# Six stack transfers a group in place of twelve: heads innermost in the scratch, stack rows ordered by part

## The chip, the cores and the metric

One core of one Trainium2 chip runs the whole program. The metric is device time in microseconds (us) of that core, the median of several executions.

## The reference

Eight sequences of 512 rows with 256 features pass through an attention layer and a mixture-of-experts layer, each followed by a layer norm. Cut to what matters here:

```python
qkv = (x @ qkv_w.T + qkv_b).reshape(B, T, 3, H, dh)          # B 8, T 512, H 16, dh 16
q, k, v = ...                                                # (B, H, T, dh) each
scores = where(causal, -inf, einsum('bhtd,bhsd->bhts', q, k) * dh ** -0.5)
seq_out = einsum('bhts,bhsd->bhtd', softmax(scores), v)
gated = mean over heads of sigmoid(memory_score * mem_scale) * sigmoid(x @ memg_w.T + memg_b)
x = layernorm(x + (seq_out + gated * mem_val) @ out_w.T + out_b)
x = layernorm(x + top2_experts_of_8(x))                      # float32 throughout
```

The memory score is a decayed running sum over products of "lines" computed from x; it is a side path of the kernel that runs on POOL and DVE.

## The kernel before, in words

**Arithmetic of the scores.** Float32 accuracy comes out of bf16 matmuls: q and k are each split into three bf16 parts (0 the coarsest), and of the nine products of parts six are kept. They are summed by the contraction itself. For one head the tile `Q` holds 96 rows (`STACK`): 16 features times six copies, where `Q_PARTS` names the part of q in each copy; `K` has the same rows with `K_PARTS`. One 96-row matmul of `Q` against `K` then gives the score. In `Q` two more rows, 96 and 97, hold the row maxima as two bf16 parts, against rows of -1 in `K`, so the transposed scores come out with the maximum already taken off.

**Projection.** For batch b+1, PE computes eight slices j (`pe_project`, L382). j = 0 to 3 are 128 channels of q or k each, (64 channels, or four heads, are one group; q of groups 0 and 1 is j = 0, k of them j = 1, and j = 2, 3 are groups 2 and 3). ACT writes part 0 into `HL` (L427), DVE the rest into `R` (L501), ACT part 1 (L438), POOL part 2 (`pool_third`, L632). SP stores the 128 x 3 x 512 bf16 slice in DRAM, `qk_scratch` (`sp_projected`, L642). j = 4 to 7 are v and memory values; the latter are stored by L645.

**Stacking.** `sp_stack` (L647 to L657) reads the scratch back, once for each copy: for tensor t (0 for Q, 1 for K) and each of six copies r it fills rows r, r+6, r+12, ... of the tile, 16 rows of four heads of 512 values. That is twelve transfers of 64 KB a group. It waits until the exp scores of the same group in the batch before are done (`s_st`), because they read the rows that it overwrites, and until the slice has landed in the scratch (`s_scr`).

**Attention.** A batch has four groups g, and a group has twelve units u. For each unit PE does the "exp scores" (L334: transposed scores with the maximum off), which ACT turns into probabilities (L419), POOL masks (L626) and PE multiplies with V (L345). Eight units ahead PE does the "max scores" (L322), and DVE takes the masked maximum of each row (L491). When the maxima of a group are complete, PE turns them (L365), ACT and DVE split them into `MT` (L452, L507), and SP copies `MT` into rows 96 and 97 of `Q` (`sp_max_rows`, L662). The first exp score of a group waits for these (`s_mrow`).

**Order on SP.** Every transfer of the program is issued by SP, in an order written out by hand (`sp_batch`). Beside the compute of batch b: in g = 0 the stack of group 3 of b, the load of x for b+2, MT of (b,1), slice 0 of b+1; in g = 1 the Q stack of (b+1,0), slice 1, MT of (b,2), the K stack of (b+1,0), slice 2; in g = 2 the stack of (b+1,1), slices 3 and 4, MT of (b,3), slice 5; in g = 3 the stack of (b+1,2), slice 6, MT of (b+1,0), slice 7. The semaphore of each piece is waited for in this order, so a late piece holds up what follows.

**Opening and end.** Before batch 0 (`opening`) PE projects batch 0 and all sixteen tiles of the memory lines (L238); SP stores these (L275), loads further x, stores the slices, and issues all four stacks of batch 0, then MT of (0,0). After batch 7 a third part, without any stack, does the output projection, norms and experts (`phase3`, PE L1296).

Of the kernel before, what the change touches and what calls it, by code (L numbers as in the profile page):

```python
# [8 lines left out]
BF16 = mybir.dt.bfloat16  # L9
# [5 lines left out]
P = 128  # L15
# [2 lines left out]
LEAD = 8  # L18
GROUP = 4
STACK = 96  # L20
Q_PARTS, K_PARTS = (0, 0, 1, 1, 0, 2), (0, 1, 0, 1, 2, 0)
TERMS = len(Q_PARTS)
VW = 17
NEG = -1e30
EPS = 1e-5
# [7 lines left out]
def need(eng, sem, per, b, c, least=1, apart=False):  # L33


    if isinstance(b, int):
        if per * b + c > 0:
            eng.wait_ge(sem, per * b + c)
    else:
        assert per * least + c > 0  # L40
        value = eng.to_reg(b * per + c)
        if apart:
            eng.wait_ge(sem, 1)
        eng.wait_ge(sem, value)


def build(nc, xT, x, qk_wT, qk_b, vc_wT, memv_w, memv_bT, out_wT, mem_wT, v_b, memg_b, mem_scale, decay_logits,
          iter_mix, out_b, gate_wT, gate_b, expert_w, expert_b, out):
    NB, _, KT, T = xT.shape
    D = KT * P  # L50
    QT = T // P
    H = memg_b.shape[0] // NB
    DH = D // H
# [5 lines left out]
    PU = NG * UNITS  # L59
    assert (NB, KT, T, H, DH, NG, NE) == (8, 2, 512, 16, 16, 4, 8)  # L60

    qk_scratch = nc.dram_tensor("qk_scratch", [NB, 4, P, 3, T], BF16, kind="Internal").ap()
    mem_scratch = nc.dram_tensor("mem_scratch", [NC, NB, H, T], F32, kind="Internal").ap()
    mv_scratch = nc.dram_tensor("mv_scratch", [NB, QT, P, D], F32, kind="Internal").ap()
    o_scratch = nc.dram_tensor("o_scratch", [NB, QT, P, D], F32, kind="Internal").ap()
# [1 line left out]
    with ExitStack() as ctx:  # L67
        def sb(name, shape, dt=F32, scope=ctx):
            return scope.enter_context(nc.sbuf_tensor(name, shape, dt))

        def sem(name):
            return ctx.enter_context(nc.semaphore(name))
# [41 lines left out]
        HL = sb("HL", [P, 2, 3, T], BF16, part2)  # L114
        Q = sb("Q", [P, H, T], BF16, part2)
        K = sb("K", [P, H, T], BF16, part2)
# [55 lines left out]
        s_scr = [sem(f"s_scr{i}") for i in range(4)]  # L172
        s_mvst = [sem(f"s_mvst{i}") for i in range(2)]
        s_stack = [sem(f"s_stack{i}") for i in range(NG)]
# [117 lines left out]
        def unit_parts(u):  # L292

            if u < 4:
                return 0, [u]
            if u < 8:
                return 1, [u - 4]
            return (2, [2 * (u - 8), 2 * (u - 8) + 1]) if u < 10 else (3, [2 * (u - 10), 2 * (u - 10) + 1])
# [13 lines left out]
        def pe_max_scores(pe, b, g, u):  # L312
            rank, heads = unit_parts(u)
            i = QT - 1 - rank
            n = P * (i + 1)
            if u == 0:
                need(pe, s_stack[g], 32 * TERMS, b, 32 * TERMS)
            need(pe, s_max, PU, b, UNITS * g + u - 2)
            for c, h in enumerate(heads):
                hh = GROUP * g + h  # L320
                o = S_ps[u % 3][:, c * 256:c * 256 + n]
                last = nc.tensor.matmul(o, Q[0:STACK, hh, P * i:P * i + P], K[0:STACK, hh, 0:n], start=True, stop=True)  # L322
            last.then_inc(s_s, 1)
# [65 lines left out]
        def pe_batch(pe, b, first=False, last=False):  # L389
            for g in range(NG):  # L390
                pb, pg = (b, g - 1) if g else (b - 1, NG - 1)
                for u in range(UNITS):
                    pe_exp_scores(pe, b, g, u)
                    on, ng, nu = ahead(g, u)
                    if not (last and on):
                        pe_max_scores(pe, b + on, ng, nu)
                    if u in (2, 6) and not (first and g == 0):
                        for kt in ((0, 1) if u == 2 else (2, 3)):
                            pe_values(pe, pb, pg, kt)
                    if u in (4, 10) and not last:  # L400
                        pe_project(pe, b + 1, 2 * g + u // 10)
                    if u == UNITS - LEAD and not (last and g == NG - 1):
                        pe_turn_max(pe, b + (g + 1) // NG, (g + 1) % NG)
                    if u == 10 and not (first and g == 0):
                        pe_turn_out(pe, pb, pg)
                    if last and (g, u) == (2, 8):
                        pe_gates(pe)
                    if last:
                        last_phase["tensor"]["beside"](pe, g, u)
# [229 lines left out]
        def sp_projected(sp, b, j):  # L639
            if j < 4:  # L640
                need(sp, s_h3, 4, b, j + 1, apart=True)
                sp.dma_start(qk_scratch[b, j], HL[:, j % 2]).then_inc(s_scr[j], 16)  # L642
            else:
                need(sp, s_hi, 8, b, j + 1, apart=True)
                sp.dma_start(mv_scratch[b, j - 4], MV[:, j % 2, :]).then_inc(s_mvst[j % 2], 16)  # L645

        def sp_stack(sp, b, g, which=(0, 1)):  # L647

            need(sp, s_st, PU, b, UNITS * (g + 1) - PU, apart=True)
            r0 = GROUP * DH * (g % 2)  # L650
            for t in which:
                j = 2 * (g // 2) + t
                need(sp, s_scr[j], 16, b, 16, apart=True)
                src = qk_scratch[b, j][r0:r0 + GROUP * DH].rearrange("(h d) s t -> s d h t", h=GROUP)
                for r, part in enumerate((Q_PARTS, K_PARTS)[t]):
                    sp.dma_start((Q, K)[t][r:STACK:TERMS, GROUP * g:GROUP * g + GROUP, :],  # L656
                                 src[part]).then_inc(s_stack[g], 16)  # L657

        def sp_max_rows(sp, b, g):
            need(sp, s_mt, 2 * NG, b, 2 * (g + 1), apart=True)  # L660
# [8 lines left out]
        def sp_batch(sp, b, first=False, last=False, more=True, read_rows=None):  # L669
            for g in range(NG):  # L670
                if g == 0 and not first:
                    sp_stack(sp, b, NG - 1)
                if g == 1 and not last:
                    sp_stack(sp, b + 1, 0, (0,))
                if g > 1 and not last:
                    sp_stack(sp, b + 1, g - 1)
                if g in (1, 2) and not last:
                    sp_projected(sp, b + 1, 2 * g - 1)
# [5 lines left out]
                if g > 1 and not last:  # L684
                    sp_projected(sp, b + 1, 2 * g)
# [4 lines left out]
                if not last:  # L690
                    sp_projected(sp, b + 1, 2 * g + (g > 1))
# [334 lines left out]
        def _(pe):  # L1026
# [20 lines left out]
            def scores(u0):  # L1047
                if u0 == 0:
                    for c in range(2):
                        pe.wait_ge(s_p1e[c], 3)  # L1050
                    pe.wait_ge(s_wr, 4)
                for u in range(u0, u0 + 3):
                    pe_max_scores(pe, 0, 0, u)
# [6 lines left out]
            for u in range(LEAD):  # L1060
                pe_max_scores(pe, 0, 1, u)
# [623 lines left out]
```

## Time and profile before

| | us |
|---|---|
| median of 3 runs (821.67 to 824.83) | 822.56 |
| the profiled execution, its own time | 823.05 |
| span of the profiled execution | 821.3 |
| PE busy (share of span) | 687.0 (84%) |
| DVE busy | 586.8 (71%) |
| POOL busy | 453.3 (55%) |
| ACT busy | 367.2 (45%) |
| granted TensorE clock, mean | 0.938 |
| stack transfers: 192 to Q and 192 to K, 64 KB each, issue to landing | 2.3 each |

PE is the matmul engine, PEld its weight load, DVE, ACT and POOL the three elementwise engines; SPq is the queue from which SP issues transfers. A transfer is issued by SP, cut into packets by hardware and moved by 16 DMA engines; "landing" is when its completion is seen. Busy shares are averages over stages with different limits: where one engine waits for another is read from the timelines and the chain.

### The profile page before, as it was taken

How to read it: one execution, taken by the hardware profiler on the slowest of the kernel's cores; microseconds unless marked ns; L12 is line 12 of the kernel's file. 1: busy time of each engine (PE TensorE's matmuls, PEld its weight loads, DVE VectorE, ACT ScalarE, POOL GpSimd, SP SyncE). 2: the span in 40 equal slices, each digit the busy share in tenths (PEclk: the TensorE clock that was granted, in tenths of full speed). 3: DMA queues.
4: the chain of work that ended last, by engine and by line, in shares of the span. 5: the costliest groups of instructions: out<-in, count | busy, mean ns of one | idle time of the engine just before them, and what ended most of it. 6: DMA issues, size and time to landing. Idle time of an engine off the chain costs nothing.

```text
span 821.3 us, 12578 instructions
## 1 busy us (share of the span) xinstructions
PE 687.0 (84%) x4004; PEld 421.6 (51%) x4004; DVE 586.8 (71%) x1946; ACT 367.2 (45%) x790; POOL 453.3 (55%) x365
## 2 busy tenths in 40 slices
PE   5992877978887888888888887779999899998995
PEld 2440443434444444444444442547677677776774
DVE  2443755956989887988888676546778777787785
ACT  3311644645656555655556465633323242232411
POOL 5200599998887786978987971514224043151410
PEclk9996898989999999999999997888999999999998
DMA  7665435233443332433433436030230311303000
GB/s 251 210 220 156 164 114 187 94 110 92 130 129 112 109 112 85 139 109 120 135 85 98 125 104 193 1 103 4 74 103 1 102 42 62 103 1 103 26 27 26
DMA packets 75445, 85.44 MB, mean 104 GB/s; under 512 B 11994, under 2 KB 64628, under 8 KB 75380
## 3 DMA queue, kind: packets, MB, share of 16 engines
q1 hardware_dynamic: 75380, 84.64, 32.9%
q8 instruction: 32, 0.52, 0.3%
q14 instruction: 33, 0.27, 0.1%
HBM read 54.72 MB, written 29.62 MB: 103 GB/s over the span
## 4 chain that ended last, share of the span: by engine, by line
PE 37%; DVE 22%; SPq 12%; POOL 12%; ACT 6%; issue 6%; DMA 4%; ACTq 0%; POOLq 0%; DVEq 0%
PE ps L1296 16%; SPq L656 9%; PE ps L382 5%; DVE ps L491 4%; PE ps L345 4%; PE ps L334 4%; DVE Ob L530 3%; DVE A L1430 3%; PE ps L322 2%; PE ps L1261 2%; ACT Pr L419 2%; POOL Pr L626 2%; ACT X L1282 2%; DMA Q<-MT 1%; DVE Z L1316 1%
## 5 line engine op out<-in xcount | busy, mean ns | idle before, releaser
L491 DVE CUSTOM_DVE_ANT_0 ps<-ps,mask 128x256 f32<-128x256 f32 (+3 forms) x512 | 237.8, 511 | 109.8 <-PE ps L322 108.3
L419 ACT ACTIVATE Pr<-ps 128x512 f32<-128x512 f32 (+2 forms) x384 | 183.9, 522 | 95.1 <-PE ps L334 94.1
L334 PE MATMUL ps<-Q,K 98*128 98x256 bf16 (+3 forms) x512 | 141.0, 320 | 61.1 <-DMA Q<-MT 34.8
L1296 PE MATMUL ps<-ew_hi,XT 128*128 128x512 f32 x512 | 176.6, 403 | 0.0
L322 PE MATMUL ps<-K,Q 96*128 96x256 bf16 (+3 forms) x512 | 138.6, 317 | 27.1 <-DVE nmax L491 26.2
L626 POOL TENSOR_SCALAR_AFFINE_SELECT Pr<-Pr 128x512 f32<-128x512 f32 x128 | 95.9, 763 | 113.2 <-ACT Pr L419 111.9
L1430 DVE SCALAR_TENSOR_TENSOR A<-ps,cw,A 128x256 f32<-128x256 f32 x256 | 123.6, 483 | 47.6 <-PE ps L1296 34.8
L334 PEld LDWEIGHTS ps<-Q,K 98*128 98x128 bf16 x512 | 46.0, 101 | 137.8 <-ACT Pr L419 68.7
L1296 PEld LDWEIGHTS ps<-ew_hi,XT 128*128 128x128 f32 x512 | 97.3, 190 | 21.1 <-issue 0.3
L1234 POOL TENSOR_TENSOR A<-A,X 128x512 f32<-128x512 f32 x16 | 20.6, 1288 | 149.3 <-ACT A L1288 149.3
L1296 PE MATMUL ps<-ew_rest,XT 128*128 128x512 f32 x256 | 101.7, 397 | 0.0
L345 PE MATMUL ps<-Pr,V 128*17 128x512 f32 (+3 forms) x1024 | 90.0, 471 | 0.2
L322 PEld LDWEIGHTS ps<-K,Q 96*128 96x128 bf16 x512 | 51.9, 103 | 63.7 <-issue 23.8
L491 DVE DVE_READ_ACCUMULATOR2_ANT nmax<- 128x1 f32 x512 | 70.3, 137 | 0.0
L1296 PEld LDWEIGHTS ps<-ew_rest,XT 128*128 128x128 f32 x256 | 48.7, 190 | 8.6
L632 POOL TENSOR_TENSOR HL<-R,HL 128x512 bf16<-128x512 f32 x32 | 38.9, 1215 | 25.2 <-ACT HL L438 24.2
L530 DVE TENSOR_TENSOR_SCAN Ob<-sc,Ob 128x512 f32<-128x512 f32 x36 | 49.8, 1383 | 1.0 <-POOL Ob L876 1.0
L382 PE MATMUL ps<-xhi,wqk 128*128 128x512 f32 x128 | 47.2, 453 | 3.2 <-DVE xlo L524 3.2
L345 PEld LDWEIGHTS ps<-Pr,V 128*17 128x17 f32 x1024 | 24.2, 101 | 48.8 <-issue 34.1
L427 ACT ACTIVATE HL<-ps,qkb 128x512 bf16<-128x512 f32 x32 | 22.0, 687 | 58.9 <-PE ps L382 52.2
L382 PE MATMUL ps<-wvc,xhi 128*128 128x512 f32 x128 | 45.2, 434 | 1.1 <-DVE bc L986 1.1
L882 POOL TENSOR_TENSOR Ob<-Ob,Rl 128x1533 f32<-128x1533 f32 x12 | 34.8, 2903 | 18.2 <-DVE Ob L530 18.2
(191 smaller groups left out, 1095.9 us busy)
## 6 DMA issues: line engine op xcount, KB each, us to landing
qk_scratch<-HL SPq DMA_DIRECT2D x32, 384.0 KB, 2.6
Q<-qk_scratch SPq DMA_DIRECT2D x192, 64.0 KB, 2.3
K<-qk_scratch SPq DMA_DIRECT2D x192, 64.0 KB, 2.3
Pr<-xT SPq DMA_DIRECT2D x8, 512.0 KB, 5.7
xraw<-xT SPq DMA_DIRECT2D x8, 512.0 KB, 3.8
mem_scratch<-Rl SPq DMA_DIRECT2D x16, 256.0 KB, 3.4
mv_scratch<-MV SPq DMA_DIRECT2D x32, 128.0 KB, 2.1
Wm<-mem_scratch SPq DMA_DIRECT2D x2, 2048.0 KB, 9.2
```

The lines of the kernel that those rows point to most:

```text
L322: last = nc.tensor.matmul(o, Q[0:STACK, hh, P * i:P * i + P], K[0:STACK, hh, 0:n], start=True, stop=True)
L334: last = nc.tensor.matmul(o, K[0:STACK + 2, hh, P * kt:P * kt + P], Q[0:STACK + 2, hh, T - n:T], start=True, stop=True)
L345: last = nc.tensor.matmul(O_ps[32 * h:32 * h + VW, P * kt:T], V[b % 2][:, kt, GROUP * g + h, :], probs(g % 2, kt, h, 1)[:, 0, :], start=(k ...
L382: last = nc.tensor.matmul(J_ps[:], lhs, rhs, start=first, stop=(j < 4 and k == KT - 1 and a == 1))
L419: nc.scalar.activation(probs(g % 2, kt, heads[0], len(heads)), src, ACT.Exp, scale=SCALE).then_inc(s_exp, 1)
L491: last = nc.vector.tensor_tensor_reduce(out=scores, in0=scores, in1=mask[:, T - w:T], scale=1.0, scalar=NEG, op0=ALU.add, op1=ALU.max, acc ...
L530: nc.vector.tensor_tensor_scan(Ob[:, j % 3, :], col(SC_D).to_broadcast([P, T]), Ob[:, j % 3, :], 0.0, ALU.mult, ALU.add).then_inc(s_scan, 1)
L626: nc.gpsimd.affine_select(out=diagonal, in_=diagonal, compare_op=ALU.is_ge, fill=0.0, base=0, pattern=[[0, GROUP], [1, P]], channel_multip ...
L632: nc.gpsimd.tensor_tensor(HL[:, j % 2, 2, :], R[:, j % 2, :], HL[:, j % 2, 1, :], ALU.subtract).then_inc(s_h3, 1)
L656: sp.dma_start((Q, K)[t][r:STACK:TERMS, GROUP * g:GROUP * g + GROUP, :], src[part]).then_inc(s_stack[g], 16)
L1296: last = nc.tensor.matmul(o, lhs(c, k), rhs(d, k), start=first, stop=(k == KT - 1 and c == 1))
L1430: ins = nc.vector.scalar_tensor_tensor(acc, F_ps[v % 4][:, D * c:D * c + D], cw[:, par, i, e:e + 1], acc, ALU.mult, ALU.add)
```

## The change

The scratch gets the part index outermost, so that a part of a slice is a block of 128 rows of 512 values. The host reorders the weight rows and biases of q and k, so that within a group the feature comes first and the head last: four heads of one feature are then 4 KB in one piece. The stack's rows are ordered by part (Q: part 0 three times, part 1 twice, part 2 once, 16 rows each; K: parts 0, 1, 2, then 0, 1, then 0), which are the same six products. For each of Q and K one transfer now fills 48 rows, one 32 and one 16. Q's repeats its source block 3, 2 and 1 times, K's reads 3, 2 and 1 consecutive blocks. The store into the scratch has rows of 1 KB in the scratch in place of 3 KB.

```diff
--- before.py
+++ after.py
@@ -18,8 +18,7 @@
 LEAD = 8
 GROUP = 4
 STACK = 96
-Q_PARTS, K_PARTS = (0, 0, 1, 1, 0, 2), (0, 1, 0, 1, 2, 0)
-TERMS = len(Q_PARTS)
+TERMS = ((0, 3), (1, 2), (2, 1))
 VW = 17
 NEG = -1e30
 EPS = 1e-5
@@ -59,7 +58,7 @@
     PU = NG * UNITS
     assert (NB, KT, T, H, DH, NG, NE) == (8, 2, 512, 16, 16, 4, 8)
 
-    qk_scratch = nc.dram_tensor("qk_scratch", [NB, 4, P, 3, T], BF16, kind="Internal").ap()
+    qk_scratch = nc.dram_tensor("qk_scratch", [NB, 4, 3, P, T], BF16, kind="Internal").ap()
     mem_scratch = nc.dram_tensor("mem_scratch", [NC, NB, H, T], F32, kind="Internal").ap()
     mv_scratch = nc.dram_tensor("mv_scratch", [NB, QT, P, D], F32, kind="Internal").ap()
     o_scratch = nc.dram_tensor("o_scratch", [NB, QT, P, D], F32, kind="Internal").ap()
@@ -314,7 +313,7 @@
             i = QT - 1 - rank
             n = P * (i + 1)
             if u == 0:
-                need(pe, s_stack[g], 32 * TERMS, b, 32 * TERMS)
+                need(pe, s_stack[g], 96, b, 96)
             need(pe, s_max, PU, b, UNITS * g + u - 2)
             for c, h in enumerate(heads):
                 hh = GROUP * g + h
@@ -639,7 +638,7 @@
         def sp_projected(sp, b, j):
             if j < 4:
                 need(sp, s_h3, 4, b, j + 1, apart=True)
-                sp.dma_start(qk_scratch[b, j], HL[:, j % 2]).then_inc(s_scr[j], 16)
+                sp.dma_start(qk_scratch[b, j].rearrange("s p t -> p s t"), HL[:, j % 2]).then_inc(s_scr[j], 16)
             else:
                 need(sp, s_hi, 8, b, j + 1, apart=True)
                 sp.dma_start(mv_scratch[b, j - 4], MV[:, j % 2, :]).then_inc(s_mvst[j % 2], 16)
@@ -651,10 +650,13 @@
             for t in which:
                 j = 2 * (g // 2) + t
                 need(sp, s_scr[j], 16, b, 16, apart=True)
-                src = qk_scratch[b, j][r0:r0 + GROUP * DH].rearrange("(h d) s t -> s d h t", h=GROUP)
-                for r, part in enumerate((Q_PARTS, K_PARTS)[t]):
-                    sp.dma_start((Q, K)[t][r:STACK:TERMS, GROUP * g:GROUP * g + GROUP, :],
-                                 src[part]).then_inc(s_stack[g], 16)
+                src = qk_scratch[b, j][:, r0:r0 + GROUP * DH].rearrange("s (d h) t -> s d h t", h=GROUP)
+                row = 0
+                for part, n in TERMS:
+                    dst = (Q, K)[t][row:row + n * DH, GROUP * g:GROUP * g + GROUP, :]
+                    parts = src[part:part + 1].to_broadcast([n, DH, GROUP, T]) if t == 0 else src[0:n]
+                    sp.dma_start(dst, parts).then_inc(s_stack[g], 16)
+                    row += n * DH
 
         def sp_max_rows(sp, b, g):
             need(sp, s_mt, 2 * NG, b, 2 * (g + 1), apart=True)
@@ -1652,13 +1654,14 @@
     B, T, D = x.shape
     H = L0_attn_memg_b.shape[0]
     qkv_w, qkv_b = np.asarray(L0_attn_qkv_w), np.asarray(L0_attn_qkv_b)
+    turned = np.arange(2 * D).reshape(2 * H // GROUP, GROUP, D // H).transpose(0, 2, 1).reshape(-1)
     lines = [np.stack([np.asarray(w).reshape(H, 4, D) for w in two], 1).reshape(8 * H, D)
              for two in ((L0_attn_w1w, L0_attn_w2w), (L0_attn_r1w, L0_attn_r2w))]
     arrays = {
         "xT": lay(x.transpose(0, 2, 1).reshape(B, D // P, P, T).transpose(0, 2, 1, 3)),
         "x": lay(x.reshape(B, T // P, P, D)),
-        "qk_wT": lay(qkv_w[:2 * D].T),
-        "qk_b": lay(qkv_b[:2 * D].reshape(4, P).T),
+        "qk_wT": lay(qkv_w[turned].T),
+        "qk_b": lay(qkv_b[turned].reshape(4, P).T),
         "vc_wT": lay(qkv_w[2 * D:].T),
         "memv_w": lay(np.asarray(L0_attn_memv_w)),
         "memv_bT": lay(np.asarray(L0_attn_memv_b).reshape(D // P, P).T),
```

## Rows read from the trace of the kernel before

**Rows 1.** The page: span, busy share of PE, chain that ended last

```profile
PE 687.0 (84%) x4004; PEld 421.6 (51%) x4004; DVE 586.8 (71%) x1946; ACT 367.2 (45%) x790; POOL 453.3 (55%) x365
...
PE ps L1296 16%; SPq L656 9%; PE ps L382 5%; DVE ps L491 4%; PE ps L345 4%; PE ps L334 4%; DVE Ob L530 3%; DVE A L1430 3%; PE ps L322 2%; PE ps L1261 2%; ACT Pr L419 2%; POOL Pr L626 2%; ACT X L1282 2%; DMA Q<-MT 1%; DVE Z L1316 1%
```

**Rows 2.** The chain from 25 to 82 us, its summary by line

```profile
by line: SPq L656 53.8%; SPq L275 12.0%; issue 8.2%; SPq L645 4.2%; SPq L279 3.6%; PE ps L238 3.0%; DMA Q<-MT 3.0%; SPq L285 2.3%; DVE xlo L524 2.2%; POOL HL L632 2.0%; ACT xhi L457 1.9%; ACT HL L438 1.1%; PE ps L334 1.1%; SPq L662 1.0%; SP
```

**Rows 3.** Timeline of PE: start, us, engine, line, names, count, [idle before <-releaser]

```profile
79.53 0.61 PE L334 MATMUL ps<-Q,K 98*128 98x512 bf16 x1 [11.40 <-DMA Q<-MT]
...
139.28 0.61 PE L334 MATMUL ps<-Q,K 98*128 98x512 bf16 x1 [4.21 <-DMA Q<-MT]
...
186.51 0.58 PE L334 MATMUL ps<-Q,K 98*128 98x512 bf16 x1 [1.85 <-DMA Q<-MT]
...
240.99 0.39 PE L334 MATMUL ps<-Q,K 98*128 98x512 bf16 x1 [0.97 <-DMA Q<-MT]
...
298.44 0.61 PE L334 MATMUL ps<-Q,K 98*128 98x512 bf16 x1
...
354.21 0.39 PE L334 MATMUL ps<-Q,K 98*128 98x512 bf16 x1 [1.68 <-DMA Q<-MT]
...
408.50 0.39 PE L334 MATMUL ps<-Q,K 98*128 98x512 bf16 x1 [0.98 <-DMA Q<-MT]
...
465.56 0.39 PE L334 MATMUL ps<-Q,K 98*128 98x512 bf16 x1 [2.78 <-DMA Q<-MT]
...
490.26 0.55 PE L334 MATMUL ps<-Q,K 98*128 98x512 bf16 x1 [1.90 <-DMA Q<-MT]
```

**Rows 4.** Timeline of SP's queue, same columns

```profile
77.14 1.22 SPq L662 DMA_DIRECT2D Q<-MT  x2
...
225.37 3.79 SPq L656 DMA_DIRECT2D K<-qk_scratch  x6
...
280.13 3.80 SPq L656 DMA_DIRECT2D K<-qk_scratch  x6
...
392.83 3.80 SPq L656 DMA_DIRECT2D K<-qk_scratch  x6
...
406.08 1.21 SPq L662 DMA_DIRECT2D Q<-MT  x2
...
447.60 3.80 SPq L656 DMA_DIRECT2D K<-qk_scratch  x6
```

**Rows 5.** By stretch, groups 2, 3 of batch 5: PE, PEld, DVE, ACT, POOL

```profile
393.52:408.50 14.98, 12.09 (x84) 6.14 (x83) 13.49 (x43) 8.40 (x21) 13.02 (x7) 1.00 0.45 143
408.50:420.72 12.22, 11.46 (x83) 6.41 (x84) 9.62 (x33) 6.94 (x17) 9.64 (x9) 1.00 0.31 86
```

**Rows 6.** Line L656, its Q transfers: issue ns min/median/max

```profile
L656 SPq DMA_DIRECT2D Q<-qk_scratch x192: 555/596/1723, 29.9 to 483.4; - x192
```

**Rows 7.** Line L662, the transfers of MT: issue to landing

```profile
DMA to landing us min/median/max: 1.6/1.7/7.2
```

**Rows 8.** Transfer view, whole span: packets, and the transfers of few rows

```profile
DMA packets 75445, 85.44 MB, mean 104 GB/s; under 512 B 11994, under 2 KB 64628, under 8 KB 75380
...
eb_raw<-expert_b SPq DMA_DIRECT2D x3, 8.0 KB
eb_raw<-out_b SPq DMA_DIRECT2D x2, 1.0 KB
```

**Rows 9.** Transfer view, 145.2 to 146.1 us: an xT load alone

```profile
DMA packets 82, 0.34 MB, mean 373 GB/s; under 512 B 0, under 2 KB 0, under 8 KB 82
...
q1 hardware_dynamic: 82, 0.34, 93.9%
```

**Rows 10.** Transfer view, 29.5 to 41 us: busy tenths, packets

```profile
DMA  9899999999999999999471520262424333256999
...
DMA packets 1707, 2.79 MB, mean 243 GB/s; under 512 B 272, under 2 KB 1040, under 8 KB 1706
...
q1 hardware_dynamic: 1706, 2.77, 72.1%
```

## The prediction

> **What bounds the kernel now.** I read the page first. PE is busy 84% of the span, and the chain that ended last is PE with one queue in it: SP's issue of line 656 holds 9% [rows 1]. A queue's issue is on a chain only where SP is late, so I asked where. The chain from 25 to 82 us says it: line 656 has 53.8% of that stretch [rows 2]. SP issues 48 stack transfers one behind another, gets to the first row maxima (MT) at 77.14 us, and PE, which had stopped 11.40 us before, starts the exp scores at 79.53 [rows 3, 4]. In the batches PE's timeline shows the same wait with smaller numbers, mostly at the start of g = 3: 1.85, 0.97, 1.68, 0.98 and 2.78 us in batches 1, 2, 4, 5, 6, none in batch 3; also 4.21 at batch 1's start and 1.90 at (7,1) [rows 3]. Between these waits PE is nearly full (11.46 of 12.22 us in group 3 of batch 5 [rows 5]). So the kernel is bound by PE with SP's order just beside it: MT of (5,3) is issued at 406.08, its second half some 0.6 us later, and PE starts at 408.50 [rows 3, 4]. Whoever shortens or lengthens what lies ahead of MT on SP and its rings moves these points and little else. Nothing after batch 7 is touched.
>
> **The change, part by part.** *Fewer issues.* An issue of line 656 takes 0.596 us [rows 6], so a group costs SP 6 x 0.6 = 3.6 us less. This is a gain only where MT was behind the stack. In the opening 24 x 0.6 = 14.3 us fall away, more than the 11.40 that PE waits. Behind stack issues are also the waits of 4.21, 1.85, 0.97, 1.68, 0.98 and 1.90. The wait of 2.78 in batch 6 has, in SP's listing, an idle stretch of SP for POOL's part 2 of slice 3 just ahead, so I give it nothing. The most to be won is 11.40 + 4.21 + 1.85 + 0.97 + 1.68 + 0.98 + 1.90 = 23.0 us.
>
> *Larger packets.* Alone, an xT load moved 82 packets of 4 KB in 0.9 us at 93.9% of 16 engines: 16 x 0.9 x 0.939 / 82 = 0.165, and I take 0.16 us a packet for one engine, or 26 KB a us [rows 9]. Packets of mixed sizes (1.6 KB on average) took 16 x 11.5 x 0.721 / 1707 = 0.078 us each [rows 10]. A 1 KB packet is thus between 0.04 (a quarter of 0.16) and 0.078. The stack's volume is unchanged; the store's 24 packets of 1 KB on each engine cost 1.0 to 1.9 us in place of 1.0 for eight of 3 KB. I take 1.0, since the 0.078 holds waiting too; the other end adds 0.9 to a store that mostly lies beside other work.
>
> *How many engines carry a transfer.* This decides. Before, the leading index of each stack transfer, on both sides, has 16 values (the features). After, the source's leading index is the copy or the part, with 3 values, then 2; only the third transfer, where it is 1 and drops out, leads with 16 again. What the trace has on this: packets under 512 B number 11,994, and by the code 2,176 of them are data (1,024 of MT, 384 of the gate's weights and biases, 512 scalars, 256 of two small biases). The other 9,818 are completion writes. The program issues 617 transfers; 16 each would make 9,872. The 54 missing are just those of the few-row transfers: three of 8 rows lack 8 each, two of one row lack 15 each [rows 8]. So a transfer runs on as many engines as its leading index gives, up to 16. No row shows 48 destination rows under a leading 3; I carry the count over. If it holds, the first transfer runs on 3 engines with 16 packets each and the second on 2 with 16 each, and the engine that has both, with 1 of the third, has 33 packets: 33 x 0.16 = 5.3 us for one tensor, 10.6 for Q and K, where 12 transfers of 4 KB an engine took 12 x 0.16 = 1.9 us of each engine. I assume that the shared engine is the same one each time; every 16-row transfer uses it too, and MT, whose 16 packets lie one on each engine, comes in last behind it.
> The Trainium skill (DMA: Bandwidth & Descriptors, "Why a DMA increments its semaphore by 16 and not by 1" and "Rules for kernel authors") says the same more sharply: the engine count is the largest up to 16 that divides the slowest dimension of both sides, on the lowest-numbered engines, and a leading broadcast of c copies confines a transfer to at most c. By that rule, the trace's 54 missing writes agree; the 3 and 2 here are its consequence, which no run here shows yet.
>
> *What that does to MT.* A small transfer takes 1.7 us to land [rows 7], 0.1 more to PE: I put 1.8 us of fixed time on the path of issue, packets and landing. That MT waits behind its ring is in the trace: one took 7.2 us [rows 7], the one behind the 2 MB load at 129 us. In g = 2 the path begins with the K stack of (b+1,0), issued at 392.83 in batch 5, 15.7 us before group 3 starts [rows 3, 4]. On the busy engine there follow K, then Q and K of group 1 (3 x 5.3 = 15.9), the store of slice 3 (1.0), one 8 KB share of values (0.3), then MT: 15.9 + 1.0 + 0.3 + 1.8 = 19.0 us. Before, that distance was 15.6 (batch 2), 18.3 (3), 15.7 (5), 18.0 (6) [rows 3, 4], and 16.9 and 16.2 in batches 1 and 4; mean 16.8. The six lose 6 x 2.2 = 13.2 us. Batch 0 had 19.9 (POOL was late) and loses nothing. In g = 3: 10.6 + 0.3 + 1.8 = 12.7 us against a group of 12.22 [rows 5]; four batches are like this (11.8 to 12.3), the others longer: 4 x 0.6 = 2.4 us. In g = 0: 10.6, an x load of 1.3 and 1.8 make 13.7, under the group's 14.6, no loss; batch 7, without the x load, has 12.4 against 11.4: 1.0 us.
>
> *The opening.* The engines were busy without a gap until slice 19 of the view, 35.0 us, with about 1.5 us of stack in it [rows 10]. From 33.5 the busy engine then has 4 x 10.6 = 42.4 us of stacks, eleven line stores of 16 KB (6.9), three x loads (3.8), four value stores (1.2), gates (0.3): it ends at 88.1, and with 0.8 of landing PE starts at 88.9 in place of 79.53: 9.4 us later.
>
> **Sum.** 9.4 + 13.2 + 2.4 + 1.0 = 26.0 us. The profiled execution took 823.05, so 849; it stands 0.5 above the median of 822.56, which I leave. The gain of fewer issues is not added, since at each of those points MT is now held by the ring. Moved work elsewhere is nothing: the host's reordering is outside the time, and matmuls are the same in number and shape.
>
> **Rivals.** *All 16 engines carry every stack transfer*, or the starting engine rotates, so that the load evens out. Then nothing replaces SP and the 23.0 us are won: 800; with some handed to the next wait (DVE's maxima), 800 to 808. For it: the destination has 48 or 32 rows, both multiples of 16, and 54 writes speak of transfers whose rows could not be spread further. Against it: for the source the leading count is what differs. It decides where a tensor's ring time, 5.3 us in my forecast, falls under (16.8 - 3.1) / 3 = 4.6 us in g = 3 and 4.1 in the opening; 16 engines give under 1 us. *The ring is the limit, but a lone engine is quicker than in a full load*: at 0.13 us a packet a tensor takes 4.3, MT of g = 3 comes after 12.9 + 3.1 = 16.0 us, before PE wants it, and the opening ends at 33.5 + 34.4 + 12.2 + 0.8 = 80.9. That gives 1.4 us of loss against one or two of gain: 823. Against it: the 0.16 was nearly the packets' own time. *The ring saturates*: in a batch the busy engine has 4 x 10.6 of stacks and 8 of other transfers, 50 of 55 us. If its idle gaps cannot be used because SP waits for POOL, a group nears 15 us: 31 x 1.2 = 37 and the opening's 9.4 make 870, up to 885 with the dearer stores.
>
> **Chances.** My forecast with its saturated form 0.75, the 16-engine rival 0.18, the quick engine 0.07. A measurement of this kernel tells about 0.5% (4 us) from no change. Faster 0.18, same 0.07, slower 0.75. The range leaves out the fast rival alone: from 820 (the quick engine) to 885.
>
> **What would show it.** Right: the issues of line 656 number 192; their time to landing is 4 us or more, growing to 10 behind a neighbour; completion writes fall from 9,818; the mean share of the 16 engines hardly changes while GB/s in stack stretches falls to a few tens; PE's waits for Q<-MT grow at g = 3 and at 89 us; PE's busy time stays. Wrong: landings of 2 to 3 us and MT issued some 10 us sooner in the opening, PE waiting for it no more. If landings are long but MT lands early, the shared engine was assumed wrongly.

## The result, and the profile after

| | before | after |
|---|---|---|
| median, us | 822.99 (821.67 to 824.83, 4 runs) | 887.45 (885.63 to 888.4, 4 runs) |
| ratio, 95% interval | | 1.0779 (1.0749 to 1.0809) |
| span of the profiled execution | 821.3 | 886.6 |
| granted TensorE clock, mean | 0.938 | 0.908 |

The change makes the kernel 7.8% slower. The direction was that of the forecast (849), and so was the mechanism at the places that it named, but the loss is two and a half times as large as its 26 us, and the time lies 2 us beyond the range. In the tables here an execution in the chip's slower state (one of seven of e8_split_three, one of four of e11_k_confined) is left out.

The changed kernel's page, against [rows 1, 8]. The chain by line now has two DMA entries where SP's issue stood:

```profile
PE 705.0 (80%) x4004; PEld 425.4 (48%) x4004; DVE 587.6 (66%) x1946; ACT 367.5 (41%) x790; POOL 450.4 (51%) x365
...
DMA packets 60404, 85.41 MB, mean 96 GB/s; under 512 B 7194, under 2 KB 47540, under 8 KB 60340
...
q1 hardware_dynamic: 60340, 84.62, 29.6%
...
PE 37%; DVE 21%; DMA 17%; POOL 10%; ACT 6%; issue 5%; SPq 4%; ACTq 0%; POOLq 0%; DVEq 0%
PE ps L1298 14%; DMA Q<-MT 11%; PE ps L344 6%; PE ps L381 5%; PE ps L333 4%; DVE ps L490 4%; PE ps L321 3%; DMA K<-qk_scratch 3%; DVE A L1432 3%; DVE Ob L529 2%; PE ps L1263 2%; ACT Pr L418 2%; ACT X L1284 2%; SPq L658 2%; DMA mv_scratch<-MV 1%
```

Waiting for Q<-MT is 11% of the chain (1% before) and SP's stack issue 2% (9% before). PE's and DVE's work is the same in number; what grew is waiting, and 18 us of PE's busy time through a lower clock.

The engine count can be read from the first DMA line. Packets under 512 B fell from 11,994 to 7,194, and 2,176 of them are data as before, which leaves 5,018 completion writes. The program now issues 617 - 192 = 425 transfers. Were each of the 64 tensors' first transfers on 3 engines and the second on 2, they would lack 13 and 14 writes: 425 x 16 - 54 - 64 x 27 = 5,018, exactly. The 3 and the 2 that the prediction carried over from [rows 8] are so. The Trainium skill (DMA: Bandwidth & Descriptors, "Why a DMA increments its semaphore by 16 and not by 1") states that a transfer runs on the largest number of engines, up to 16, that divides the slowest dimension of both its sides, and that each of these engines writes one completion; this trace agrees to the last write.

The timeline of PE in the changed kernel (columns as in [rows 3]), the opening and batch 5:

```profile
46.16 1.44 PE L321 MATMUL ps<-K,Q 96*128 96x512 bf16 x3 [7.16 <-DMA K<-qk_scratch]
...
92.93 0.61 PE L333 MATMUL ps<-Q,K 98*128 98x512 bf16 x1 [16.51 <-DMA Q<-MT]
...
434.05 0.61 PE L333 MATMUL ps<-Q,K 98*128 98x512 bf16 x1 [3.02 <-DMA Q<-MT]
...
454.33 0.39 PE L321 MATMUL ps<-K,Q 96*128 96x512 bf16 x1 [1.90 <-DMA K<-qk_scratch]
...
467.86 0.61 PE L333 MATMUL ps<-Q,K 98*128 98x512 bf16 x1 [5.06 <-DMA Q<-MT]
```

The first exp score comes at 92.93 us in place of 79.53. Group 3 of batch 5 waits 5.06 us for MT where it had waited 0.98 [rows 3]. New is the wait for the K stack: 7.16 us once in the opening, and in the middle of g = 2 in six of the batches, 17.1 us together. Against the trace of before, the starts of the 32 groups account for the loss so: 13.4 us before the first group; 31.5 in the seven intervals from g = 2 to g = 3 (19.3 us in batch 5, from 448.57 to 467.86, against 14.98 [rows 5]); 10.8 from g = 3 to the next batch (14.92 against 12.22 [rows 5]); 13.4 in the others. That is 69.1.

The last part took 295.5 us in place of 299.2, though it has no stacks. The difference goes with its first 38 us (columns as in [rows 5], then granted clock, DMA share, GB/s; the kernel before, then the changed one):

```profile
522.13:560.00 37.87, 28.75 (x172) 19.30 (x173) 16.38 (x58) 15.71 (x34) 14.29 (x15) 0.80 0.18 56
```

```profile
591.17:629.04 37.87, 29.77 (x191) 18.97 (x192) 19.18 (x65) 17.15 (x37) 17.49 (x15) 0.87 0.18 56
```

TensorE's granted clock has a mean of 0.80 there in one and of 0.87 in the other, and more of the work gets done in the same time. The last part is about as short in every run below (295.1 to 296.8 us) but one, e9_first_mt_act, which has 0.80 and 299.3 us. But e6_mt_act has 0.81 and 296.8, so the clock isn't all of it. What makes the difference is open; as it does not follow the engines that carry the stacks, I do not count these 3.7 us to them.

SP's queue in batch 5 of the changed kernel, from the K stack of (6,0) on (columns as in [rows 4]; it was read in two windows that meet at 450, so Q's three issues stand in two lines):

```profile
445.61 2.25 SPq L658 DMA_DIRECT2D K<-qk_scratch  x3
447.92 0.56 SPq L641 DMA_DIRECT2D qk_scratch<-HL  x1
448.60 1.38 SPq L658 DMA_DIRECT2D Q<-qk_scratch  x2
450.03 0.96 SPq L658 DMA_DIRECT2D Q<-qk_scratch  x1
451.04 1.83 SPq L658 DMA_DIRECT2D K<-qk_scratch  x3
452.92 0.42 SPq L641 DMA_DIRECT2D qk_scratch<-HL  x1
456.78 0.34 SPq L644 DMA_DIRECT2D mv_scratch<-MV  x1
458.79 1.19 SPq L664 DMA_DIRECT2D Q<-MT  x2
```

MT is issued at 458.79 us and PE starts 9 us later. The transfer view of the changed kernel shows where it is, in three stretches, 459.9 to 461.2, 461.2 to 463 and 466 to 467.6 us:

```profile
DMA packets 73, 0.07 MB, mean 56 GB/s; under 512 B 58, under 2 KB 58, under 8 KB 72
...
q1 hardware_dynamic: 72, 0.06, 16.2%
```

```profile
q1 hardware_dynamic: 23, 0.09, 11.9%
```

```profile
DMA packets 85, 0.10 MB, mean 63 GB/s; under 512 B 14, under 2 KB 76, under 8 KB 85
...
q1 hardware_dynamic: 85, 0.10, 17.4%
```

Both halves of MT are 32 packets of 256 B. By their sizes in the packet record, 28 of them run in the first stretch, and the last four at 467.0. Between these, 11.9% of 16 engines is busy: 1.9 engines, moving 4 KB packets one after another, with fourteen idle. MT has landed for fourteen sixteenths and waits for the two engines that still have stacks ahead of it. The first packet of the K stack starts at 447.15, and from then on the packet record shows two engines' time or more taken in every half microsecond until MT's last packet.

### The profile page after: what moved, and what is told of

It reads as the page before. It is cut to its first block, busy times and chain, and to the rows that moved or that the text cites. A ratio compares the mean times of both kernels' runs of the same rounds, so it can differ in the third digit from the quotient of the medians.

```text
span 886.6 us, 12386 instructions
## 1 busy us (share of the span) xinstructions
PE 705.0 (80%) x4004; PEld 425.4 (48%) x4004; DVE 587.6 (66%) x1946; ACT 367.5 (41%) x790; POOL 450.4 (51%) x365
## 2 busy tenths in 40 slices
DMA packets 60404, 85.41 MB, mean 96 GB/s; under 512 B 7194, under 2 KB 47540, under 8 KB 60340
## 3 DMA queue, kind: packets, MB, share of 16 engines
q1 hardware_dynamic: 60340, 84.62, 29.6%
## 4 chain that ended last, share of the span: by engine, by line
PE 37%; DVE 21%; DMA 17%; POOL 10%; ACT 6%; issue 5%; SPq 4%; ACTq 0%; POOLq 0%; DVEq 0%
PE ps L1298 14%; DMA Q<-MT 11%; PE ps L344 6%; PE ps L381 5%; PE ps L333 4%; DVE ps L490 4%; PE ps L321 3%; DMA K<-qk_scratch 3%; DVE A L1432 3%; DVE Ob L529 2%; PE ps L1263 2%; ACT Pr L418 2%; ACT X L1284 2%; SPq L658 2%; DMA mv_scratch<-MV 1%
## 5 line engine op out<-in xcount | busy, mean ns | idle before, releaser
L333 PE MATMUL ps<-Q,K 98*128 98x256 bf16 (+3 forms) x512 | 146.0, 330 | 96.2 <-DMA Q<-MT 69.4
L625 POOL TENSOR_SCALAR_AFFINE_SELECT Pr<-Pr 128x512 f32<-128x512 f32 x128 | 90.9, 722 | 172.2 <-ACT Pr L418 171.1
L321 PE MATMUL ps<-K,Q 96*128 96x256 bf16 (+3 forms) x512 | 143.3, 327 | 41.6 <-DMA K<-qk_scratch 24.3
L344 PE MATMUL ps<-Pr,V 128*17 128x512 f32 (+3 forms) x1024 | 99.8, 514 | 0.1
L321 PEld LDWEIGHTS ps<-K,Q 96*128 96x128 bf16 x512 | 53.9, 106 | 80.9 <-issue 33.8
L381 PE MATMUL ps<-wvc,xhi 128*128 128x512 f32 x128 | 48.8, 465 | 1.1 <-DVE bc L988 1.1
```

The source lines that it names most:

```text
L333: last = nc.tensor.matmul(o, K[0:STACK + 2, hh, P * kt:P * kt + P], Q[0:STACK + 2, hh, T - n:T], start=True, stop=True)
L344: last = nc.tensor.matmul(O_ps[32 * h:32 * h + VW, P * kt:T], V[b % 2][:, kt, GROUP * g + h, :], probs(g % 2, kt, h, 1)[:, 0, :], start=(k ...
L381: last = nc.tensor.matmul(J_ps[:], lhs, rhs, start=first, stop=(j < 4 and k == KT - 1 and a == 1))
L625: nc.gpsimd.affine_select(out=diagonal, in_=diagonal, compare_op=ALU.is_ge, fill=0.0, base=0, pattern=[[0, GROUP], [1, P]], channel_multip ...
```

## The experiments

Each ran beside the kernel before on the same chip, whose median there was 820.0 to 821.0 us. In this table "packets" are the 4 KB packets of one group's Q and K on its busiest engine. The code is cut to the lines that matter: where the number of transfers changes, the count that PE waits for changes with it.

| run | stack transfers a group | packets | median, us | ratio to before (95%) |
|---|---|---|---|---|
| changed kernel | 6, on 3, 2, 16 engines | 66 | 887.45 | 1.0779 (1.0749 to 1.0809) |
| e1_feature_first | 6, on 16 | 12 | 808.23 | 0.9845 (0.9776 to 0.9913) |
| e1b_feature_first, the same again | 6, on 16 | 12 | 807.44 | 0.9824 (0.9787 to 0.9861) |
| e2_twelve_4k | 12, on 16 | 12 | 810.32 | 0.9882 (0.9845 to 0.9918) |
| e3_split_two | 8, on 3 and 16 | 38 | 821.38 | 1.0017 (0.9982 to 1.0052) |
| e8_split_three | 10, on 2 and 16 | 40 | 828.77 | 1.0089 (1.0053 to 1.0125) |
| e4_q_confined | Q 3, K 6 | 39 | 832.28 | 1.0156 (1.0084 to 1.0228) |
| e11_k_confined | Q 6, K 3 | 39 | 842.95 | 1.0283 (1.0184 to 1.0382) |
| e6_mt_act | 6, on 3, 2, 16; MT on ACT's queue | 66 | 858.8 | 1.0474 (1.0425 to 1.0523) |
| e10_stores_pool | as e6, stores on GpSimd's queue | 66 | 862.46 | 1.0514 (1.0448 to 1.058) |
| e9_first_mt_act | as e1, MT on ACT's queue | 12 | 819.85 | 0.9979 (0.9949 to 1.001) |
| e7_warm | changed kernel, extra matmuls | 66 | 886.53 | 1.0807 (1.0754 to 1.086) |

**The source's index order alone.** Everything of the change stays but the order in which a transfer walks its source:

```diff
-src = qk_scratch[b, j][:, r0:r0 + GROUP * DH].rearrange("s (d h) t -> s d h t", h=GROUP)
+src = qk_scratch[b, j][:, r0:r0 + GROUP * DH].rearrange("s (d h) t -> d s h t", h=GROUP)
-parts = src[part:part + 1].to_broadcast([n, DH, GROUP, T]) if t == 0 else src[0:n]
+parts = src[:, part:part + 1].to_broadcast([DH, n, GROUP, T]) if t == 0 else src[:, 0:n]
```

> The changed kernel with one thing altered: source index order feature, copy, head, value in place of copy, feature, head, value, so that each of the six transfers leads with 16 values; rows of Q and K are permuted alike. Packets stay 4 KB, transfers six, Q's repeats stay. Theory A (a transfer runs on as many engines as its leading index gives, and MT waits behind the ring of the busiest): the 3 and 2 engines become 16, completion writes under 512 B rise from 7,194 by 27 x 64 = 1,728 to 8,922, and the 23 us of waits behind SP's issues fall away: 800 to 808 us. Theory B (repeated reads of one block, or the new scratch layout, make it slow): it stays above 850.

Measured: 808.23 us, with this page:

```profile
PE 681.6 (84%) x4004; PEld 415.8 (51%) x4004; DVE 589.8 (73%) x1946; ACT 367.6 (45%) x790; POOL 449.4 (56%) x365
...
DMA packets 62132, 85.42 MB, mean 106 GB/s; under 512 B 8922, under 2 KB 49268, under 8 KB 62068
...
q1 hardware_dynamic: 62068, 84.63, 34.6%
```

The 8,922 small packets are those expected to the last one; the time is 0.2 us above what I expected. The same bytes, data packets, repeats and number of transfers give 808 or 887 us, by the leading index of the source. Theory B falls with this one run: Q's repeated reads and the new layout are all still there, and the loss is gone. The share of q1 goes the other way from what one might think: 34.6% in the fast kernel, 29.6% in the slow one. It is a mean over 16 engines, and shows nothing of two that are full.

It was timed a second time in more rounds:

> The same kernel as e1_feature_first, timed in more rounds. Both theories expect its first result again, 804 to 811 us, faster than the kernel before by 1 to 2%.

807.44 us, 1.8% below the kernel before (1.4 to 2.1): this version beats both.

**Layout and packets without the fewer transfers.** Each part and copy in its own transfer of 16 rows:

```diff
+for part, n in TERMS:
+    for c in range(n):
+        dst = (Q, K)[t][row:row + DH, GROUP * g:GROUP * g + GROUP, :]
+        sp.dma_start(dst, src[c if t else part]).then_inc(s_stack[g], 16)
+        row += DH
```

> The changed layout and row order with twelve transfers of 16 rows each, no repeats. Against the kernel before only the packets of the stack (4 KB for 1 KB) and of the store (1 KB for 3 KB) differ. Theory A: SP issues as many as before, so 818 to 826 us. Theory B with the layout at fault: above 830.

810.32 us, faster than expected. The issues of the stack in this run, and in the feature-first one (line L658, ns min/median/max; compare [rows 6]):

```profile
L658 SPq DMA_DIRECT2D Q<-qk_scratch x192: 302/420/1787, 29.5 to 472.4; - x192
```

```profile
L658 SPq DMA_DIRECT2D Q<-qk_scratch x96: 551/581/1434, 29.7 to 472.1; - x96
```

With the new layout an issue got cheaper: a transfer of 64 packets of 1 KB took SP 0.596 us [rows 6], one of 16 packets of 4 KB 0.420. The number of packets is not all of it: in e1_feature_first the transfers of 48, 32 and 16 packets took 0.563, 0.593 and 0.580 us at the median, so 16 packets cost 0.580 there and 0.420 here. What sets the time of an issue isn't shown. Twelve issues fell from 7.2 to 5.0 us a group, and six cost 3.5. Most of the good of this change comes with the layout (10 us of the 12 to 14), not with the count of transfers. The prediction had priced all issues at 0.6.

**Less load on the busiest engine.** In the first of these runs the 32-row transfer becomes two of 16 rows, in the second the 48-row one becomes three; in the other two, one of the tensors goes in six transfers of 16 rows.

```diff
-for part, n in TERMS:
-    dst = (Q, K)[t][row:row + n * DH, GROUP * g:GROUP * g + GROUP, :]
+for part, n in TERMS:
+    for c, m in (((0, 3),) if n == 3 else ((0, 1), (1, 1)) if n == 2 else ((0, 1),)):      # e3
+    for c, m in (((0, 1), (1, 1), (2, 1)) if n == 3 else ((0, n),)):                       # e8
+        dst = (Q, K)[t][row:row + m * DH, GROUP * g:GROUP * g + GROUP, :]
```

> The changed kernel with the 32-row transfer cut into two of 16 rows: eight transfers a group, the busiest engine has 16 + 3 = 19 packets or 3.0 us for a tensor in place of 5.3. Theory A: that is under the 4.1 and 4.6 us at which the ring begins to hold MT, and SP saves four issues a group, so the loss is gone: 802 to 820 us. A rival by which each confined transfer costs time in proportion to its bytes on few engines (16 of 32 excess packets remain): about 855.

> The changed kernel with the 48-row transfer cut into three of 16 rows and the 32-row one kept (on 2 engines): ten transfers a group, 16 + 4 = 20 packets on the busiest engine against 19 in the run that kept the 48-row one on 3 engines. If the busiest engine's packets decide, it is within 4 us of that run (821): 817 to 826. If the number of engines a transfer has (2 against 3) decides, it is clearly slower, 835 or more.

821.38 and 828.77 us, with intervals that just do not overlap. The first is just beyond what I expected (820). The second is beyond its 826 too, and short of the 835 by which the number of engines would decide. It is nearer to the packets' answer, but the two runs don't settle it: 828.77 has two transfers a group more to issue as well. The loss is gradual. Against 810, 38 packets cost 11 us, 40 cost 18, 66 cost 77. My threshold of 4.1 to 4.6 us of ring for a tensor, under which there would be no loss, is not there: at 3.0 us PE waits 31.1 us for MT, against 22.7 with all stacks on 16 engines (e2_twelve_4k) and 15.9 (e1_feature_first), and 10.4 us for the K stack, against none in both. The wait view of e3_split_two (total us, times, longest us):

```profile
PE ps L333 <- DMA Q<-MT: 31.1, 11, 5.8
...
PE ps L321 <- DMA K<-qk_scratch: 10.4, 6, 3.2
```

> Q as in the changed kernel (3, 2 and 16 engines, repeats), K in six transfers of 16 rows: nine a group. Theory A: a pair takes 5.3 + 1.0 = 6.3 us of the busiest engine, MT at g = 3 comes 1.0 + 5.3 + 1.0 + 2.4 + 1.8 = 11.5 us after the K stack's start, under 16.8, and the opening is bound by SP with 12 issues fewer: 805 to 820. The proportional rival: half of the 64 us, 855. Theory B with repeats at fault: all of the loss stays, 880.

> The mirror of e4_q_confined: Q in six transfers of 16 rows, K in three whose source leads with 3, 2 and 16, without any repeated source. The busiest engine has the same 33 + 6 = 39 packets a pair. If packets on the busiest engine decide, it is within 6 us of 832. If Q's repeated reads of one block had a cost of their own, it is clearly under 822.

832.28 and 842.95 us. The first is neither the 805 to 820 of theory A nor half of the loss. With equal packets, K confined is the dearer, 11 us apart where I allowed 6, though it has no repeated source; the ranges of the times are apart (830.06 to 835.85, 838.81 to 848.52), but the intervals of the ratios overlap. So no price of the repeats shows. That place has one fits the waits: of the next batch's first group, Q is issued early in g = 1 and K only before g = 2, which needs it. The wait view of e11_k_confined:

```profile
PE ps L321 <- DMA K<-qk_scratch: 28.8, 8, 5.2
...
PE ps L333 <- DMA Q<-MT: 26.2, 10, 8.8
```

With Q confined PE waits for K once, 4.0 us in the opening, and for MT 45.9 us in 16 places.

**MT past the ring.** MT goes out on ACT's queue, behind unit 6 (`...` stands for the same index as in the kernel):

```diff
+def act_max_rows(act, b, g):
+    need(act, s_mt, 2 * NG, b, 2 * (g + 1))
+    for r in range(2):
+        act.dma_start(Q[STACK + r:STACK + r + 1, ...], MT[:, g % 2, r, :]).then_inc(s_mrow[g], 16)
-                if not (last and g == NG - 1):
-                    sp_max_rows(sp, b + (g + 1) // NG, (g + 1) % NG)
```

> The changed kernel with MT's transfers (rows 96 and 97 of Q) issued from ACT's queue in place of SP's, after unit 6; the stacks stay on 3, 2 and 16 engines in SP's queue. Theory A (MT waits behind SP's ring of the busiest engine): with a ring of its own MT lands about 2 us after it is ready, the 69.4 us of PE waits for Q<-MT fall to the 10 or 15 that POOL's lateness leaves, the 24 us of waits for K stay or grow: 830 to 850 us. Rival (the engine's load itself, or the issuing path shared by both queues, holds MT): MT still lands late and the time stays above 875.

858.8 us, above my range and below the rival's. The issuing queue has a control, the same move in the feature-first kernel:

> The feature-first kernel (16 leading values) with MT issued from ACT's queue. If what is left of PE's waits for MT there (15.9 us, three places behind a slice that POOL finishes late) is on the path, 795 to 802 us. If POOL's lateness itself is on the path, through the slices that the next batch needs, it stays at 804 to 812.

819.85 us, above both ranges. There MT on ACT's queue costs 12 us of its own. In the profiled executions it is not lost in the batches: the first exp score comes 5.4 us later than in e1_feature_first (72.35 against 66.96), from there to the last group it is 447.2 us against 447.0, and the last part takes 299.3 against 295.3, with the clock of 0.80 named above. Between these two, then, the confined stacks cost 39 us, and with MT in SP's queue 79 (808 to 887). So about half of the loss goes through MT. In e6_mt_act PE's wait for MT is nearly gone, and the stacks themselves and the slice stores are late:

```profile
PE ps L321 <- DMA K<-qk_scratch: 25.6, 7, 7.4
ACT HL L426 <- DMA qk_scratch<-HL: 23.6, 6, 6.7
...
PE ps L333 <- DMA Q<-MT: 6.3, 6, 2.2
```

**Stores past the ring too.** On top of e6_mt_act, GpSimd issues each slice store behind its own part 2, and SP no longer does:

```diff
+            need(pool, s_h3, 4, b, j + 1, apart=True)
+            nc.gpsimd.dma_start(qk_scratch[b, j].rearrange("s p t -> p s t"), HL[:, j % 2]).then_inc(s_scr[j], 16)
```

> The changed kernel (3, 2 and 16 engines) with MT on ACT's queue, as in e6_mt_act, and the slice stores issued by GpSimd right behind its part 2, on a third queue. Theory (after MT, the stores' shares behind the stacks on the two busy engines hold up HL and the K stack): ACT's 23.6 us of waits for the slice stores fall under 8, the K stack is issued earlier, and the 859 fall to 825 to 845. Rival (the stacks' own 10.6 us a group on two engines is the rest): ACT's waits for stores fall but PE's waits for K take their place, and the time stays above 852.

862.46 us: no gain. ACT's waits for the stores fell only to 17.5 us, PE's for K to 20.3. The rival has it as far as the time goes, though not by its own account, for the waits did not change places. It speaks for the stacks' own time as the rest. A queue of its own freed the stores only in part: they landed after 4.6 us at the median, against 7.1 in e6_mt_act and 2.6 in e1_feature_first. In the packet record the last packets of a late one (4 KB each in this queue, not 1 KB) start 0.31 us apart on an engine (301.7 to 302.7 us), twice the 0.16 that one takes, so they alternate with the stacks' packets there. How the remaining 39 us divide between that and the stacks stays open.

**The clock.** PE had 18 us more of busy time. By stretch, groups 1 to 3 of batch 5 of the changed kernel (columns as in [rows 5], then granted clock, DMA share, GB/s):

```profile
434.05:448.57 14.52, 13.63 (x81) 6.78 (x82) 8.00 (x32) 8.01 (x17) 10.42 (x7) 0.78 0.33 100
448.57:467.86 19.29, 12.06 (x85) 6.15 (x83) 13.97 (x43) 8.33 (x21) 14.31 (x12) 0.99 0.34 119
467.86:482.78 14.92, 14.40 (x84) 7.22 (x85) 9.42 (x32) 7.11 (x17) 5.60 (x4) 0.78 0.15 53
```

Behind the stalls of 3.02 and 5.06 us the granted clock of the group is 0.78 (a mean over the two levels, 1.2 and 2.4 GHz); in group 3 it had been 1.00 [rows 5], and PE needs 14.40 us for what took 11.46. To see whether these 2 to 3 us a group are a second loss, PE was kept busy during the stall:

```diff
+            need(pe, s_exp, PU, b, UNITS * g + u - 1)
             if u == 0:
+                for _ in range(14 if g == 3 else 0):
+                    nc.tensor.matmul(ST_ps[0][:, 0:n], K[0:STACK, GROUP * g, 0:P], Q[0:STACK, GROUP * g, 0:n],
+                                     start=True, stop=True)
                 need(pe, s_mrow[g], 32, b, 32)
-            need(pe, s_exp, PU, b, UNITS * g + u - 1)
```

> The changed kernel with 14 extra matmuls of 512 columns, whose result is overwritten, in front of PE's wait for MT at g = 3 (about 3 us of PE at full clock, inside the stall of 2.5 to 5.4 us; in batches 0 to 6; batch 7 has no stall there and pays 3 us). Theory (the second part of the loss is TensorE's clock, which falls to the lower level after a stall: groups after it take 14.3 us in place of 12.2): the group after g = 3's stall takes 12.2 to 13 us again at a granted clock near 1.0, and the whole is 4 to 10 us shorter: 877 to 883. Rival (the groups are longer because transfers are late): the group lengths stay above 14 and the time is 887 to 895.

The clock did what was expected. Group 3 in batches 3, 4 and 5 of e7_warm:

```profile
338.38:350.21 11.83, 11.31 (x84) 6.40 (x85) 7.36 (x31) 6.95 (x17) 8.65 (x5) 1.00 0.19 69
402.59:414.85 12.26, 11.63 (x85) 6.32 (x84) 10.41 (x35) 7.36 (x18) 6.01 (x3) 1.00 0.22 73
465.58:477.67 12.09, 11.47 (x84) 6.40 (x84) 9.25 (x32) 6.94 (x17) 4.28 (x4) 1.00 0.19 68
```

The groups are back at 12 us and clock 1.00, and yet the whole takes 886.53 us, which is neither the 877 to 883 of the theory nor, by half a microsecond, the 887 of the rival. The matmuls also run in batch 7, where nothing stalls: its g = 2 to g = 3 takes 19.1 us in place of 16.2. Up to there, from group to group of the profiled executions, group 3 of batches 0 to 6 was 8.7 us shorter in all, and 5.7 of it were given back, for the seven intervals from g = 2 to g = 3 grew, in batch 5 from 19.3 to 20.7 us. From the first group to g = 2 of batch 7 it took 478.5 us in place of 482.1. So at g = 3 the lower clock cost some 3.6 us, by one execution each, which the 3.0 us for the matmuls of batch 7 nearly cancel. The rest of what it seemed to cost was taken back ahead of the next stalls, as it would be if the two engines set the pace. The groups behind the other stalls weren't tried.

## Why the prediction was right and wrong

- **How many engines carry a transfer** was right, in kind and in count: 5,018 completion writes, and 79 us between the two orders of the source.
- **MT behind the ring** was right; its size was wrong. The prediction put 19.0 us from the K stack's first issue to group 3. Measured are 21.4 to 23.1 us in the seven batches, 22.2 in batch 5. They are more even than before, when they ranged from 15.6 to 19.9, as a path through one engine would be, but 3 us longer than the sum. One term was left out: the store of slice 2 is issued between the K stack and the stack of (b+1,1), as SP's rows above show (447.92), which is 1.1 us on each engine (24 packets of 1 KB at 0.046 us). And the first packet of K ran 1.54 us after its issue, where the sum had 1.0 (its 1.8 less 0.8 for landing). The rest, 1 to 2 us, I cannot place packet by packet; in batch 5 up to 0.7 of it is in K's first packets, which took 0.36, 0.66 and 0.85 us in place of 0.16.
- **Batch 0 "loses nothing"** was wrong for the same reason: 23.1 us is more than POOL's 19.9, and it lost 4.4.
- **The sum over waits** is the step that failed. It took each point where MT is waited for alone and let the rest of the batch run as before. But g = 2 was given 13.2 us and got 31.5; g = 0 and g = 1 were given 1.0 (batch 7) and got 13.4; g = 3 was given 2.4 and got 10.8. "PE's busy time stays" was wrong with it: it rose by 18 us through the lower clock, for which the sum had no term. The stalls for the K stack were not in the sum, though the prediction placed that stack just ahead of its use. The saturated rival, which the forecast counted as its own second form, described it: 4 x 10.6 us of stacks and 8 of other transfers in a batch, of which no gap can be caught up. Batches 2 to 5 took 64 to 65 us, 16 a group, above the 15 that this rival named.
- **The opening** was given 9.4 us and lost 13.4. The prediction let SP run ahead and only the ring end late. But SP itself came to MT at 83.53 us, later than the kernel before (77.14), though it had 24 issues fewer, and 20 us later than e1_feature_first (63.52) with as few. Its issues took longer: Q's three at 67.32 us took 5.78 together, and in the opening of e1_feature_first no three took more than 2.6. The 7.16 us wait for the first K stack was not in the prediction either; how much of the loss it makes isn't shown, for e6_mt_act has it too (7.38) and starts its first exp score at 79.24.
- **Fewer issues, at most 23.0 us won**: the opening's 11.40 are real (12.6 us earlier in e1_feature_first, at 66.96 us, and 10.8 in the same kernel's second profile), the other 11.6 are not. From the first group to the last it took 447.0 and 444.2 us there, against 442.6. In the first of these, PE's waits for DVE's maxima rose from 26.2 to 37.3 us, and PE still waits for MT once for 7.3 us, behind a slice that POOL finishes late.
- **The quick engine** (820 to 823) is out: alone, the two engines moved 4 KB packets at 1.9 engines' busy time, 0.16 us each.

## What to carry to other kernels

When transfers are merged, look at the leading index of source and destination before counting packets: put a dimension that 16 divides outermost, here the feature, and keep copies and parts inside. A lower DMA share with longer landings is the sign of a transfer on few engines (29.6% against 34.6%, and slice stores that land after 5.9 us against 2.6, beside e1_feature_first); the number of small packets gives the count exactly, once the small data packets are taken off. A transfer on few engines does not only land late itself: every later transfer in the same queue, however small, lands behind it if it uses those engines (MT, issue to landing, up to 10.4 us against 1.7 alone). So price the ring through a whole batch and in issue order, not wait by wait.

## What was not expected of the hardware

The time that SP needs to issue a transfer of the same 64 KB fell from 0.596 us in 64 packets to 0.420 in 16, but it was 0.580 for 16 packets under another order of the source. PE's clock at group 3 could be held at 1.00 with 3 us of extra matmuls in the stall, and of the 8.7 us saved there 5.7 were given back in the intervals that the two busy engines set.
